# Hybrid block of delta-rule attention, feed-forward and selective scan: the places of all streams drawn anew

## The chip, the cores and the metric

The kernel runs on one core of a Trainium2 chip. The metric is the device time of one execution in microseconds. A core has a matrix engine (TensorE), VectorE, ScalarE and GpSimd for work on elements, and SyncE, which here starts the DMAs. In the profile they are PE (PEld for its weight loads), DVE, ACT, POOL and SP.

## What is computed

Four layers with residuals on x of 2 x 1024 x 256 in float32, each on a layer norm of x: a gated delta-rule attention with 16 heads, a feed-forward, a selective scan (state 16), and the same feed-forward again.

```python
# attention: per head q, k, v = silu(short_conv(x @ W)); q, k normalised
def step(S, inp):
    qt, kt, vt, gt, bt = inp
    S = S * gt[..., None]
    pred = jnp.einsum('bhk,bhkv->bhv', kt, S)
    delta = (vt - pred) * bt[..., None]
    S = S + kt[..., None] * delta[:, :, None, :]
    return (S, jnp.einsum('bhk,bhkv->bhv', qt, S))
...
x = x + attn_a(layernorm(x))            # 16 heads, 1024 steps
x = x + ffn(layernorm(x))               # silu(x Wg) * (x Wu), then Wd
x = x + attn_b(layernorm(x))            # h = dA * h + dt*u*B, y = sum(h * C)
x = x + ffn(layernorm(x))
```

## The kernel before

Time lies in two segments of 512 columns. The attention runs over 32 heads, g = 0 to 31 (16 heads of each segment). The work of a head is cut into thirteen streams: three convolutions (projection by TensorE L360, copies by ScalarE L931/932, three tap products by VectorE L670), `dots` (norms of q and k, L378, L682, L686, and `bs` in L692), `gating` (L395, L703, L986/988, L708, L992), `turn_v` (L406, L718), `products`, `inverse`, `turn_k` (L507/517, L812), `solved` (L532, L541), `out_gate` (L559), `state` (eight chunks, each L579/587 by TensorE, L842 by VectorE, L592 by TensorE, L847 by VectorE; L600 after four) and `output` (L863, L873, L617, L628, L885).

`products` works in five levels. At its start VectorE scales k by the gate (L732) and GpSimd scales q (L1165); GpSimd then makes `bm` (L1171) and `side` from `bs`. In each level TensorE multiplies (L425), then VectorE scales one half of `R` (L756, in the first level also `tot` in L747 and `kL` in L754) while GpSimd scales `kL` and the other half (L1187, L1190, L1192); VectorE cuts the result out of PSUM (L764, L766). `inverse` uses these in eight rounds of 32x32 products (L467, L487, L495) with ScalarE's copy (L1008) and VectorE's L788 and L798 between.

Each stream is a generator that yields between its steps, and it exists once for each engine with the same steps. `braid` runs the streams of an engine in the order of the places of their steps. The place of step k of a stream of head g is 100 (g + lag) + place, so 100 units are one head. Since every engine uses the same places, they set the order of the instructions in each engine's queue, and nothing else: what waits for what is in semaphores. A queue is in order, so an instruction that waits holds all that is behind it. TensorE takes its PSUM banks in turn from a ring of three, in the same order (`take`), and waits there until the bank's last reader is done.

In the last heads two feed-forward tiles (`EARLY_AT`, absolute places) are braided in. After a barrier of all engines (`all_over`) the tail begins: `tail_drive` braids four scans (100 units each, 64 items of a ScalarE exponential L1896, GpSimd's product L1987, VectorE's scan L1693 and product L1699, and TensorE's gathering L1512), four fronts that prepare them (`FRONT_FROM[u] + FRONT_AT`; L1614, L1621, L1629, L1639, L1664), and six feed-forward tiles (`FFN_FROM[w] + FFN_AT`; L1566, L1571, L1583, L1589).

```python
for stage, (lag, places) in zip(stages, PLACES):
    streams.append((stage(g), [100 * (g + lag) + at for at in places]))
...
streams.append((scan(u), [100 * (u + 1) + 100 * i / ITEMS for i in range(ITEMS)]))
streams.append((front(u), [FRONT_FROM[u] + at for at in FRONT_AT]))
```

## Time and profile before

| | us |
|---|---|
| median of 3 runs | 3098.76 (3098.74 to 3106.72) |
| the profiled execution | 3098.16 |
| its span, first to last instruction | 3096.4 |
| mean granted clock of TensorE | 0.934 of full |
| busy: PE, PEld | 2679.6 (87%), 1611.2 (52%) |
| busy: DVE, ACT, POOL | 2304.3 (74%), 1404.4 (45%), 1451.9 (47%) |

The profile gives each engine's busy time, and for the idle time in front of an instruction what ended it. "issue" there is time in which an engine waited for nothing that the profile shows. An engine's busy time counts an instruction from its start to its end, also the part in which it is held up by another engine.

### The profile page before, as it was taken

To read this page: it belongs to the slowest core of one execution; us is meant where nothing else is said; L and a number is where in the kernel's file an instruction comes from. 1 tells how busy PE (TensorE), PEld (TensorE's weight loads), DVE (VectorE), ACT (ScalarE), POOL (GpSimd) and SP (SyncE) were. 2 spreads that over 40 slices of the span, in tenths; PEclk is the share of its full clock that TensorE was granted. 3 is DMA by queue.
4 is the path that set the end of the run, shared out by engine and by line. 5 is a ranking of instruction groups with operands and counts; after the bars stand their busy time and mean duration, and the time that the engine had idled before them with its cause. 6 is when DMAs were issued, how large, how long until landed. Compare 5 with 4: busy or idle time off the path is not lost.

```text
span 3096.4 us, 119846 instructions
## 1 busy us (share of the span) xinstructions
PE 2679.6 (87%) x54704; PEld 1611.2 (52%) x54704; DVE 2304.3 (74%) x3249; ACT 1404.4 (45%) x2584; POOL 1451.9 (47%) x1245
## 2 busy tenths in 40 slices
PE   6788888988889888988988998888978889888889
PEld 3455556665666655666665666556433334333333
DVE  3677777877788877787877887775214999999992
ACT  3444444444454544454444544443326454635441
POOL 0534444444445444445444454443002887766760
PEclk8899989999899999999989999998989999989999
DMA  1000000000000000000000000001001332323330
GB/s 47 20 11 12 12 12 18 13 13 12 12 18 14 12 12 12 18 12 15 12 12 13 17 15 12 12 6 47 1 22 49 106 116 93 115 96 113 104 111 14
DMA packets 52137, 106.71 MB, mean 34 GB/s; under 512 B 7084, under 2 KB 11948, under 8 KB 51376
## 3 DMA queue, kind: packets, MB, share of 16 engines
q1 hardware_dynamic: 51632, 99.04, 9.9%
q8 instruction: 431, 7.06, 0.9%
q14 instruction: 74, 0.61, 0.1%
HBM read 96.65 MB, written 2.37 MB: 32 GB/s over the span
## 4 chain that ended last, share of the span: by engine, by line
PE 65%; DVE 16%; issue 11%; ACT 6%; DMA 0%; DVEq 0%; POOL 0%; SPq 0%; ACTq 0%; POOLq 0%
PE bank L360 10%; PE bank L467 9%; DVE hs L1693 5%; PE bank L628 4%; PE pair L592 3%; PE bank L425 3%; PE bank L395 3%; PE bank L1512 3%; DVE cv L670 3%; PE pair L579 3%; PE bank L1434 2%; PE bank L600 2%; PE bank L541 2%; PE bank L532 2%; PE pair L1434 1%
## 5 line engine op out<-in xcount | busy, mean ns | idle before, releaser
L670 DVE SCALAR_TENSOR_TENSOR cv<-raw,taps,cv 128x1024 f32<-128x1024 f32 x288 | 449.8, 1562 | 22.5 <-ACT cv L932 21.0
L1987 POOL TENSOR_TENSOR dBu<-dtu,Bn 128x512 f32<-128x512 f32 x256 | 377.8, 1480 | 62.8 <-DVE hs L1693 60.0
L360 PE MATMUL bank<-xn,W 128*128 128x512 f32 x768 | 401.1, 649 | 3.8 <-issue 3.8
L931 ACT ACTIVATE raw<-bank 128x512 f32<-128x512 f32 x192 | 114.8, 598 | 522.0 <-PE bank L360 522.0
L1190 POOL TENSOR_TENSOR kL<-kL,tot 128x512 f32<-128x512 f32 x128 | 188.5, 1473 | 345.6 <-PE bank L425 345.6
L1512 PE MATMUL bank<-hc,eye 128*128 128x512 f32 x512 | 271.2, 639 | 72.6 <-DVE hc L1699 72.0
L1896 ACT ACTIVATE bank<-dtv,m_A 128x512 f32<-128x512 f32 x256 | 173.7, 688 | 247.7 <-DVE hs L1693 243.0
L360 PEld LDWEIGHTS bank<-xn,W 128*128 128x128 f32 x768 | 144.3, 202 | 147.9 <-issue 123.6
L1512 PEld LDWEIGHTS bank<-hc,eye 128*128 128x128 f32 x512 | 93.1, 197 | 236.0 <-DVE hc L1699 158.8
L1192 POOL TENSOR_TENSOR R<-R,tot 128x512 f32<-128x512 f32 x128 | 212.5, 1661 | 0.0
L1699 DVE TENSOR_TENSOR hc<-hs,Cn 128x512 f32<-128x512 f32 x256 | 194.0, 758 | 8.8
L592 PE MATMUL pair<-vT,kT 64*128 64x128 f32 x1024 | 134.3, 341 | 43.2 <-DVE vT L842 43.2
L467 PE MATMUL bank<-XY,Z 32*32 32x32 f32 x8192 | 121.0, 206 | 57.0 <-issue 57.0
L847 DVE SCALAR_TENSOR_TENSOR Sx<-S,tot_chunk,pair 128x128 f32<-128x128 f32 x256 | 76.2, 339 | 124.9 <-PE pair L592 124.9
L1165 POOL TENSOR_TENSOR R<-qn,gate 128x1024 f32<-128x1024 f32 x32 | 77.5, 2421 | 194.3 <-ACT gate L992 194.3
L1693 DVE TENSOR_TENSOR_SCAN hs<-bank,carry,dBu 128x512 f32<-128x512 f32 x128 | 163.4, 1277 | 4.2 <-ACT bank L1896 3.3
L756 DVE TENSOR_TENSOR R<-R,tot 128x512 f32<-128x512 f32 x128 | 105.9, 827 | 78.9 <-PE bank L425 78.9
L425 PEld LDWEIGHTS bank<-R,kL 128*32 128x32 f32 x10240 | 118.3, 112 | 86.1 <-issue 78.5
L1693 DVE TENSOR_TENSOR_SCAN hs<-bank,dBu 128x512 f32<-128x512 f32 x128 | 155.7, 1216 | 8.8 <-ACT bank L1896 8.8
L425 PE MATMUL bank<-R,kL 128*32 128x64 f32 (+1 forms) x10240 | 139.9, 205 | 19.2 <-issue 8.8
L467 PE MATMUL bank<-Z,XY 32*32 32x32 f32 x8192 | 116.8, 203 | 43.7 <-issue 41.3
L592 PEld LDWEIGHTS pair<-vT,kT 64*128 64x128 f32 x1024 | 82.7, 198 | 130.5 <-DVE vT L842 63.5
(270 smaller groups left out, 6094.5 us busy)
## 6 DMA issues: line engine op xcount, KB each, us to landing
Bn<-ssm_rows SPq DMA_DIRECT2D x128, 256.0 KB, 3.5
Cn<-ssm_rows SPq DMA_DIRECT2D x128, 256.0 KB, 3.2
W<-in_head_w SPq DMA_DIRECT2D x32, 448.0 KB, 3.2
WO<-in_out_w SPq DMA_DIRECT2D x32, 192.0 KB, 2.3
xT<-in_xT SPq DMA_DIRECT2D x1, 2048.0 KB, 7.5
out_xT<-xT SPq DMA_DIRECT2D x4, 512.0 KB, 4.0
xn<-in_w_gate SPq DMA_DIRECT2D x1, 1024.0 KB, 5.7
xn<-in_w_up SPq DMA_DIRECT2D x1, 1024.0 KB, 8.5
```

The lines of the kernel that those rows point to most:

```text
L360: m = pe.matmul(psum[bank][:, :], w[:, (kind * KT + k) * P:(kind * KT + k + 1) * P], xn[:, k, b, cols], start=k == 0, stop=k == KT - 1)
L425: m = pe.matmul(o, block(kL[s], c, b, u), r)
L467: m = pe.matmul(psum[INV][quad(w), (at * NC + c) * SUBB:(at * NC + c + 1) * SUBB], lhsT[quad(w), c, :], rhs[quad(w), c, :])
L592: m = pe.matmul(psum[CHAIN[b]][:, P:2 * P], kT[s][rows_of(b), c, :], vT[g % 3][rows_of(b), c, :])
L670: dve.scalar_tensor_tensor(cv[m % 2][:, :, :], raw[m % 2][:, :, i:i + SEG], taps[:, h, KQV[n], i:i + 1], cv[m % 2][:, :, :], MUL, ADD).the ...
L1190: pool.tensor_tensor(Lv[:, :, 0, :], Lv[:, :, 0, :], spread(two[:, :, 1], 2, half), MUL).then_inc(up_l.sem)
L1192: pool.tensor_tensor(Rv[:, 1, :, 1, :], Rv[:, 1, :, 1, :], spread(two[:, :, 0], 2, half), MUL).then_inc(up_q.sem)
L1512: pe.matmul(psum[Y_BANKS[jj]][:, :], eye[:, :], hc[(u * ITEMS + i) % AHEAD][:, :], start=False, stop=n == NS - 1, skip_group_check=True).t ...
L1693: dve.tensor_tensor_scan(hs[at % NA][:, :], psum[A_BANKS[at % NA]][:, :], dBu[at % AHEAD][:, :], carry[:, b, i:i + 1] if seg else 0.0, MUL ...
L1699: dve.tensor_tensor(hc[at % AHEAD][:, :], hs[at % NA][:, :], Cn[at // DT2 % DEEP][:, :], MUL).then_inc(hc_set.sem)
L1896: act.activation(psum[A_BANKS[at % NA]][:, :], dtv[u % 2][:, j, :], ACT.Exp, scale=m_A[:, j, n:n + 1]).then_inc(dA_set.sem)
L1987: pool.tensor_tensor(dBu[at % AHEAD][:, :], dtu[s][:, j, :], Bn[at // DT2 % DEEP][:, :], MUL).then_inc(dBu_set.sem)
```

## The change

Only numbers change: the places of all thirteen attention streams, of the two early feed-forward tiles, and those of fronts and feed-forwards in the tail. The lags and the numbers of steps stay as they are. In `PLACES` the entries are, in order, the streams as listed above (convolutions of k, q, v; dots; gating; turn_v; products; inverse; turn_k; solved; out_gate; state; output). The change is described as places redrawn knowing that VectorE's two-operand SBUF products and GpSimd's instructions exclude each other.

```diff
@@
 PLACES = [
-    (0, [-1, 7.3, 19, 20.5, 26.9, 34.4]),
-    (0, [18.6, 27.2, 35.2, 42.1, 51.2, 58.1]),
-    (0, [40.1, 51.1, 52.9, 52.9, 59.8, 61.8]),
-    (0, [57.5, 62.1, 70.7, 83.3]),
-    (0, [66.3, 66.3, 70.5, 83.1, 83.8, 94.9]),
-    (0, [83, 89.7]),
-    (1, [1.4, 1.4, 2.9, 5.9, 12.5, 18.2, 28.2, 37.2, 41.7, 46.7, 57.2, 67.1, 73.2, 75.4, 78.4]),
-    (1, [13.2, 31.6, 33.3, 35.8, 39.7, 44.3, 47, 49.3, 49.4, 57.2, 59.8, 63.8, 67.2, 76.6, 76.6, 78.5, 81.5,
-         83.6, 83.9, 89.9, 94]),
-    (1, [78.5, 82.8, 83, 83]),
-    (1, [102.2, 102.5, 103.2]),
-    (2, [14.6, 16.3]),
-    (2, [10.5, 15.5, 16.4, 16.5, 20, 24.3, 29.2, 33.5, 35.6, 47.4, 51.7, 57.3, 59.8, 65.6, 69.9, 74, 78.4,
-         78.4]),
-    (2, [40.1, 40.1, 77.9, 79.2, 79.4, 82.3, 82.3, 89, 89.2, 93.2, 93.2, 98.2, 104]),
+    (0, [-8.5, 14.8, 26.1, 26.5, 30.8, 37.7]),
+    (0, [17.7, 29.9, 34.7, 36.4, 42.7, 42.9]),
+    (0, [40.6, 45.2, 57.6, 59.2, 64.4, 65.9]),
+    (0, [69.8, 71.7, 74.1, 101.1]),
+    (0, [54.3, 70.2, 79.9, 88.5, 90, 92.8]),
+    (0, [84.8, 87.3]),
+    (1, [-7.8, -5.8, 2.6, 13, 16.3, 17.1, 27, 30.8, 40.7, 43.6, 53.4, 55.2, 70.5, 73.6, 83.6]),
+    (1, [16.1, 20.3, 21.5, 30.7, 37, 42.2, 42.4, 48.8, 49.4, 56.4, 60.6, 60.6, 64.8, 71.2, 71.2, 74.3, 77.5,
+         78.6, 84.7, 89.9, 90.8]),
+    (1, [78.3, 80.4, 87.6, 91]),
+    (1, [94.4, 95.7, 100.8]),
+    (2, [11.5, 41.5]),
+    (2, [7.5, 14.1, 16.2, 17, 19.9, 26.2, 30.4, 35.9, 35.9, 47.9, 51.9, 53.6, 55.9, 57.6, 65, 71, 74.1, 75.2]),
+    (2, [31.2, 42.6, 76.4, 77.7, 81.8, 86.1, 87.8, 95.5, 96.3, 98.7, 106.3, 111.8, 119.6]),
 ]
@@
-FFN_AT = [-6.8, -5, -2.1, 1.9, 6.6, 8.8, 10.8, 17.9, 19.4, 22.5, 25.8, 39.4, 44.4, 48.1, 50.7, 53.6, 55.6, 59.8,
-          65.3, 69.1, 71.9, 75.5, 80.8, 84.2, 92.2, 99.6]
-FFN_FROM = [0, 0, 29.6, 149.1, 229.8, 347.3, 431.6, 515.9]
-FRONT_FROM = [-32.6, 87.5, 207.3, 307.1]
+FFN_AT = [-16.5, -9, -4.1, 11.5, 17.9, 21.5, 28, 28.3, 35.2, 36.9, 40.5, 47.4, 50.3, 51.9, 54.7, 55.2, 56.8, 58.5,
+          59.5, 61.4, 68, 72.6, 79.7, 91.4, 111.8, 220]
+FFN_FROM = [0, 0, 43.8, 141.1, 240, 340.5, 429.9, 519.6]
+FRONT_FROM = [-2, 102.3, 199.3, 299.2]
```

`FRONT_AT` (44 places, -11.4 to 89.8 before, -9.5 to 91.6 after) and `EARLY_AT` are replaced in the same way. In `EARLY_AT` tile 0 goes from 3306.3 to 3391.1 before, and from 3224.3 to 3447.1 after. Its sum, centring, squares and scaling stand at 3224.3 to 3260.2, its gate products at 3317.2 to 3337.4, its two down products at 3375.5 and 3382.5. Tile 1 goes from 3363.7 to 3475.4 before, and from 3355 to 3748.4 after; its eight gate products stand at 3392.4 to 3401.9 before, and from 3466.6 on after. The last step of the last head's output is at 3404 before and at 3419.6 after.

## Rows read from the trace of the kernel before

**Rows 1.** Windows of the stages: stretch, its length, each engine's busy time, clock, DMA.

```profile
62.00:2108.00 2046.00, 1798.82 (x51164) 1230.95 (x51162) 1592.93 (x2429) 961.61 (x1951) 936.57 (x793) 0.93 0.04 13
2108.00:2288.00 180.00, 159.88 (x1924) 90.03 (x1922) 64.77 (x122) 54.46 (x104) 26.34 (x21) 0.95 0.06 20
2288.00:2371.70 83.70, 56.52 (x104) 21.61 (x104) 21.63 (x29) 43.17 (x55) 8.39 (x11) 0.82 0.17 49
2371.70:2388.30 16.60, 15.45 (x32) 6.57 (x32) 6.28 (x7) 6.50 (x9) 8.14 (x6) 0.90 0.05 17
2388.30:3020.00 631.70, 539.15 (x1144) 212.68 (x1144) 587.15 (x631) 305.47 (x424) 471.63 (x404) 0.96 0.33 106
3020.00:3096.40 76.40, 69.84 (x162) 30.20 (x160) 14.56 (x21) 14.89 (x18) 0.00 (x0) 0.99 0.04 14
```

**Rows 2.** Waits of TensorE from 1000 to 2000 us: total, times, longest.

```profile
PE bank L467 <- issue: 38.8, 42, 1.8
PE pair L592 <- DVE vT L842: 21.9, 47, 1.3
PE bank L378 <- issue: 20.6, 15, 1.9
```

**Rows 3.** Timeline of TensorE: start, length, instructions, [idle before, releaser].

```profile
1019.49 0.45 PE L467 MATMUL bank<-XY,Z 32*32 32x32 f32 x30 [0.60 <-issue]
1019.87 1.98 PE L360 MATMUL bank<-xn,W 128*128 128x512 f32 x4
1021.78 0.76 PE L425 MATMUL bank<-R,kL 128*32 128x32 f32 x64
1022.47 0.44 PE L467 MATMUL bank<-XY,Bc 32*32 32x32 f32 x29
1023.26 0.50 PE L467 MATMUL bank<-XY,Bc 32*32 32x32 f32 x35 [0.34 <-issue]
...
1027.01 0.57 PE L467 MATMUL bank<-XY,Z 32*32 32x32 f32 x43 [1.81 <-issue]
...
1036.04 0.80 PE L592 MATMUL pair<-vT,kT 64*128 64x128 f32 x4 [1.32 <-DVE vT L842]
```

**Rows 4.** Windows before and behind the wait at 1036.04, columns as rows 1.

```profile
1027.00:1035.90 8.90, 6.37 (x315) 4.50 (x315) 7.54 (x8) 2.39 (x4) 4.47 (x4) 1.00 0.02 6
1036.00:1039.40 3.40, 3.36 (x140) 3.02 (x140) 3.02 (x6) 0.67 (x1) 0.00 (x0) 0.50 0.02 5
```

**Rows 5.** Groups by line and shape, VectorE: count, busy us, mean ns, idle before.

```profile
L670 DVE SCALAR_TENSOR_TENSOR cv<-raw,taps,cv 128x1024 f32<-128x1024 f32 x288 | 449.8, 1562 | 22.5 <-ACT cv L932 21.0
...
L747 DVE TENSOR_TENSOR tot<-gate 128x512 f32<-128x512 f32 x32 | 91.6, 2864 | 0.0
...
L732 DVE TENSOR_TENSOR R<-kL,gate 128x1024 f32<-128x1024 f32 x32 | 64.9, 2028 | 2.3 <-ACT gate L992 2.3
```

**Rows 6.** The instructions of L670: fastest, median and slowest, in ns.

```profile
L670 DVE SCALAR_TENSOR_TENSOR cv<-raw,taps,cv x288: 1269/1283/2194, 59.0 to 2084.5; 128x1024 f32<-128x1024 f32 x144
```

**Rows 7.** Timeline of GpSimd and VectorE around the `bm` product of one head.

```profile
1058.03 3.77 POOL L1171 TENSOR_TENSOR bm<-masks,bs 128x1536 f32<-128x1536 f32 x1
...
1059.42 2.92 DVE L747 TENSOR_TENSOR tot<-gate 128x512 f32<-128x512 f32 x1
1062.27 0.70 DVE L754 TENSOR_TENSOR kL<-kL,gate 128x512 f32<-128x512 f32 x1
```

**Rows 8.** Group by line and shape, TensorE's output product.

```profile
L628 PE MATMUL bank<-WT,WO 128*128 128x512 f32 x256 | 128.2, 623 | 0.0
```

**Rows 9.** Timeline of VectorE and ScalarE ahead of the first scan.

```profile
2363.71 1.23 DVE L1664 TENSOR_TENSOR dtv<-dtv,cen 128x1024 f32<-128x1024 f32 x1 [5.12 <-ACT cen L1882]
...
2385.73 2.69 DVE L1629 SCALAR_TENSOR_TENSOR un<-cen,m_norm,m_rstd 128x512 f32<-128x512 f32 x2
2388.35 1.21 DVE L1693 TENSOR_TENSOR_SCAN hs<-bank,dBu 128x512 f32<-128x512 f32 x1
...
2370.36 1.28 ACT L1763 ACT_TABLE_LOAD   x1
```

More of the change, by code:

```diff
@@ L54 @@
 ]
 FRONT_STEPS, FFN_STEPS = 44, 26
-FRONT_AT = [-11.4, -9.5, -6.6, -6.6, -0.4, 0.5, 6.8, 6.8, 7.5, 12.4, 14.9, 17.5, 17.9, 17.9, 18.3, 18.3, 19.4, 19.9,
-            20.6, 20.6, 21.9, 44.6, 44.6, 44.6, 44.6, 45.9, 51, 57.3, 59.6, 63.6, 64.6, 66.2, 67.9, 74.8, 75.2,
-            76.7, 77.5, 77.7, 80.6, 81.2, 85.9, 85.9, 86.4, 89.8]
-FFN_AT = [-6.8, -5, -2.1, 1.9, 6.6, 8.8, 10.8, 17.9, 19.4, 22.5, 25.8, 39.4, 44.4, 48.1, 50.7, 53.6, 55.6, 59.8,
-          65.3, 69.1, 71.9, 75.5, 80.8, 84.2, 92.2, 99.6]
@@ L61 @@
-FFN_FROM = [0, 0, 29.6, 149.1, 229.8, 347.3, 431.6, 515.9]
-FRONT_FROM = [-32.6, 87.5, 207.3, 307.1]
+FRONT_AT = [-9.5, -4, -1.2, 1.7, 4, 6.1, 8.8, 10.7, 14.4, 14.7, 15.8, 17.8, 17.8, 18.2, 18.3, 18.3, 18.3, 18.3,
+            18.5, 18.5, 18.8, 18.8, 18.8, 18.8, 18.8, 19.3, 19.9, 19.9, 26.9, 28.9, 40.3, 48.3, 52.1, 55.4, 59.2,
+            59.2, 59.2, 65.7, 67.9, 74.4, 75, 88, 90.5, 91.6]
+FFN_AT = [-16.5, -9, -4.1, 11.5, 17.9, 21.5, 28, 28.3, 35.2, 36.9, 40.5, 47.4, 50.3, 51.9, 54.7, 55.2, 56.8, 58.5,
+          59.5, 61.4, 68, 72.6, 79.7, 91.4, 111.8, 220]
```

8 rows, old and new, of the table EARLY_AT are left out of this document.

## Prediction

> **What bounds the kernel now.** I read the stages first. Thirty-two heads take most of the span, then come a drain, a short stretch up to the first selective scan, four scans, and an end [rows 1]. From 62 to 2108 us TensorE is busy 1798.8 of 2046 us (88%) and VectorE 1592.9 (78%): the matmul queue sets the pace, the other engines matter only where it waits for them. From 2388.3 to 3020 the order is reversed: VectorE is busy 587.2 of 631.7 us (93%).
>
> Second, the waits of TensorE from 1000 to 2000 us, some fifteen heads (L378, one of its gaps in each head, counts 15) [rows 2]. The two rows that name no other engine (short matmuls of L467 and L378) come to 59.4 us, 4.0 us a head; the wait for VectorE's `vT` before L592 is 21.9 us, 1.5 a head. In all TensorE idles (2046 - 1798.8)/31.4 = 7.9 us a head from 62 to 2108 us [rows 1], so some 2.4 us are left for every other wait.
>
> Third, the timeline of TensorE in one head [rows 3]. The gaps without a releaser start at 1019.49, 1023.26 and 1027.01, 3.77 and 3.75 us apart. Between the first two lie 30+4+64+29 = 127 matmuls, each with one weight load, so about 256 instructions. The queue cannot take them faster than 256 in some 3.76 us: a run of 32-column matmuls, 64 of which need 0.69 us (from 1021.78 to 1022.47), outruns it. The wait of 1.32 us for `vT` follows in the same head, and right behind it the granted clock is 0.50 for 3.4 us where it was 1.00 before, the lower of its two levels (1.2 and 2.4 GHz) [rows 4]. So a bunched idle costs more than its own length: a 3.4 us stretch at half clock does the work of 1.7 us.
>
> Fourth, what VectorE and GpSimd cost each other. L670 takes 1.56 us on the mean [rows 5], 1.28 as the median and up to 2.19 [rows 6]: 288 x 0.28 = 80 us over the run. L747 takes 2.86 us [rows 5]. In one head it starts at 1059.42 and ends only 0.54 us after GpSimd's `bm` product (1058.03 to 1061.80) has; the same shape behind it, L754, takes 0.70 [rows 7]. L732 takes 2.03 [rows 5]. All that is VectorE's time, in a stretch where VectorE has 22% to spare.
>
> **The change.** No instruction is added or removed; only places move, so every term below is a wait. I sorted the steps of each engine by their places, modulo one head, before and after.
>
> *VectorE and GpSimd within a head.* After the level products (L756 with GpSimd's L1190, L1192) the new order puts VectorE's work on PSUM (L842, L847, L764/766, L885) where a two-operand SBUF product (L670, L788) stood. That takes part of the 80 us away from L670. What counts is TensorE's 1.5 us a head before L592 [rows 2], most of it the wait at 1036.04 [rows 3]. I take half of it, -0.7 us a head; one bound is that all of it and 1 us of the other waits go (-2.5), the other is the loss of the next paragraph.
>
> *The step that sets `bs` (L692)* moves from 83.3 to 101.1, behind L732, L737 and the first L885. GpSimd has L1171 (`bm`) at 94.2 and waits there for `bs`; behind it in its queue stand `side`, the first L1192 and the next head's halo copies, and the second L425 product waits for L1192. L747 then goes ahead of `bm` and loses its stall (about 2.86 - 0.70 = 2.2 us), but L754 meets `bm` in flight, up to 3.77 us [rows 7]. TensorE's cover until it needs VectorE (L592 of chunk 0) is two L628 products of two matmuls, 4 x 0.623 = 2.5 us [rows 8], an out-gate product and L579. So 0 to 1.3 us a head; I take 0, since the two L628 do not count the other two, and TensorE still has L541 and L425 in front of L754.
>
> *TensorE's order.* Short matmuls (L425, L434, L455, L467, L378, L487, L495) are 1376 a head in both. Before, 672 lie between the second v projection and the next head's first; now 800. The longest stretch between two projections, up to the second L600, now holds 736 short ones and 68 others, 804 in all, 1608 instructions, 6.3 blocks of 256: at 3.76 us each 23.6 us, less one block's head start 19.8. Its own work is 804 x 6.37/315 = 16.3 us by the busy time of a like mix [rows 4], and some 15 if the short ones run at the 0.69 us for 64 of rows 3. That is 3.5 to 4.9 us of gaps; the other half of the head (576 short ones between four projections) then has next to none, where before the gaps of rows 3 stood. Against 4.0 now that is -0.5 to +0.9; I take the middle, +0.2. Sum for a head: -0.7 + 0 + 0.2 = -0.5, times 31 = **-15 us**; bounds -2.5-0.5 and +1.3+0.9 a head, -93 to +68.
>
> The Trainium skill (Runtime: NRT & Kernel Launch, Instruction fetch mechanics) says that instructions stream in blocks of 256 and that crossing a block is mostly hidden. The spacing of rows 3 agrees with the size of the block; that it is hidden does not hold here, by 4.0 us a head. By the page the term of TensorE's order would be nothing and the sum -0.7 a head, -22 us.
>
> *The other queues.* ScalarE's exp/ln of the gate go from 83.1 to 88.5 and the last exp from 94.9 to 92.8, the second tanh from 16.3 to 41.5; the ring of three banks is handed on in the new order. ScalarE is busy 47% of this stage [rows 1]; I cost these at nothing. If a bank comes late, a projection waits: inside the bounds above.
>
> *The drain (2108 to 2288 us, TensorE idle 20 us [rows 1]).* Feed-forward tile 0 starts at 3224 instead of 3306, so its norm chain hides. Tile 1's eight gate products go from 3392 to 3402 to behind the last head's output (3466 on): 16 matmuls of about 0.6 us, 10 us, no longer fill that head's norm, but tile 0's down products now do. I take **-4 us**, bounds -12 and +10.
>
> *From the barrier to the scans.* Before, ten steps of front(1) stood ahead of scan(0): VectorE's L1629 at 2385.73, then the first scan at 2388.35, although `dt` was ready at 2363.71 + 1.2 and ScalarE was through with silu and its table at 2371.6 [rows 9]. FRONT_FROM[1] goes from 87.5 to 102.3, so two steps stand ahead, and of tile 2 sixteen steps instead of twenty. The scan can start at about 2371.7, 16.6 us earlier. VectorE did 6.3 us of work in those 16.6 [rows 1], which moves into a stage that VectorE bounds: **-10 us**. Bounds: 0 and -16 for this, and +-10 for how the 44.5 us that VectorE idles in the scans [rows 1] change; front(1) now ends at 193.9, six units ahead of scan(1), where it had 23. The moved output stores sit later in SyncE's queue, where nothing waits for them; the order of the last 76 us is the same.
>
> Sum: 3098.16 (the profiled execution, 1.8 us above its span of 3096.4, and 0.6 below the median of 3098.76) - 15 - 4 - 10 = **3069**.
>
> **Rivals.** (A) *Only the tail moves.* TensorE's queue sets the head whatever VectorE does; VectorE's 22% of slack swallows its stalls. For it: the 59.4 us against 21.9 in rows 2. The heads stay, the drain too: 3098 - 10 = 3088, from 3075 to 3100.
>
> (B) *The stalls reach TensorE and its clock.* With the 1.3 us waits gone (1.5 us a head), the half-clock stretch of rows 4 goes too (1.7 us): 3.2 x 31 = 99, with drain and tail 113: 2985. Against it: the gaps of 1.8 and 1.3 us without a releaser stay, in a longer run.
>
> (C) *`bm` behind `bs`, in the bunched run: slower.* L754 held for the whole of `bm` and TensorE reaching L592 first: 1.3 us a head, from the point where `bm` starts after L747 and outlasts TensorE's 2.5 us; plus half of the 0.9 us of the longer run of short matmuls: 1.7 x 31 = 53 - 14 = +39: 3137, and 3124 with the first alone. For it: every cover in that place is TensorE's alone, and 736 short matmuls in one stretch.
>
> (D) *The change does not do what it says:* VectorE meets GpSimd as often as before, only elsewhere (L754 for L747). Then the time is as (A), and it counts there; the busy time of VectorE tells them apart.
>
> The Trainium skill (SBUF — State Buffer, the engine and AXI sides) has the shared port pair as an exclusive lock, held for the full instruction, which the one that starts first gets. L747, which ends 0.54 us after `bm`, agrees; by that, L754 would wait for nearly the whole of `bm`, which is (C).
>
> **How the numbers follow.** The forecast 0.40, (A) with (D) 0.22, (B) 0.13, (C) 0.25. Some 0.3%, 9 us, is what a measurement here can tell from no change: faster means under 3089.5. The forecast gives 0.37 faster and 0.03 same; (A) half and half; (B) faster; (C) 0.03 same and 0.22 slower. Together faster 0.61, same 0.17, slower 0.22. For 8 in 10 I leave out the far half of (B) and the far end of (C): 2992 to 3132.
>
> **What would show it.** L747 near 0.7 us and L754 above 1.2: the `bs` step as described. L670's mean under 1.45: the port relief is real. TensorE's wait before L592 under 1 us a head: the gain term. The gaps without a releaser 3.5 to 4.9 us a head and bunched between the v projections and L507: the block reading; fewer, and it was wrong. The first L1693 some 16 us nearer to the barrier: the tail term. I would be wrong most simply if a head's mean length changed by over 1.5 us either way.

## Result: 2976.6 us, 4% faster, below the forecast range

| | before | after |
|---|---|---|
| median, us | 3098.75 (3095.6 to 3106.72, 4 runs) | 2976.56 (2969.01 to 2989.22, 4 runs) |
| ratio | | 0.9606, 95% interval 0.9568 to 0.9644 |
| profiled execution, its span | 3098.16, 3096.4 | 2969.01, 2967.2 |
| TensorE's mean granted clock | 0.934 | 0.956 |

The forecast was 3069, with a range from 2992: the sign was right, the gain is four times the 29 us of the sum. The profiled execution of the changed kernel is the fastest of its four, at the highest clock (the median of the four is 0.9535). Lines of the changed kernel are one lower than before's (L669 is L670 of before).

The stages of the changed kernel, columns as rows 1: the heads, the drain, from the drain to the first scan, the scans, the end.

```profile
62.00:2012.00 1950.00, 1745.45 (x51056) 1185.92 (x51054) 1442.77 (x2417) 944.67 (x1929) 880.72 (x791) 0.96 0.05 14
2019.80:2201.70 181.90, 163.04 (x1937) 89.07 (x1936) 64.63 (x127) 58.94 (x111) 26.33 (x21) 0.97 0.06 20
2201.70:2281.00 79.30, 56.64 (x111) 22.35 (x112) 21.11 (x29) 45.38 (x57) 13.08 (x15) 0.85 0.19 55
2281.00:2887.30 606.30, 537.52 (x1174) 216.46 (x1173) 587.81 (x637) 313.23 (x433) 476.99 (x406) 0.98 0.34 111
2887.30:2967.20 79.90, 70.31 (x157) 29.64 (x156) 15.69 (x22) 14.89 (x18) 0.00 (x0) 0.98 0.04 13
```

Of the 129.2 us between the two spans the heads (first L434 of head 0 to first L434 of head 31, 2027.7 and 1943.3 us) carry 84, the stretch from the drain to the first scan 20 (100.5 and 80.1), the scans 23 (629.1 and 606.2) and the fill 4; drain and end are 2 and 1 us longer. In the scans, fourth line against the fifth of [rows 1], VectorE is busy 587.8 us as before, but its idle time falls from 44.5 to 18.5 us. The drain ends, and the stretch to the first scan begins, with the start of the last residual sum ahead of the tail (L1589 of before, at 2287.85 and 2201.02 us).

The waits of TensorE from 1000 to 2000 us in the changed kernel, the four longest and one more (before: [rows 2]):

```profile
PE bank L377 <- issue: 24.1, 15, 1.9
PE bank L424 <- issue: 22.8, 15, 1.9
PE bank L466 <- issue: 17.7, 19, 1.8
PE pair L591 <- DVE vT L841: 6.0, 15, 0.4
...
PE bank L466 <- DVE XY L797: 4.0, 16, 0.3
```

The wait for `vT` falls from 21.9 to 6.0 us, 0.4 us a head. The idle time that names no other engine does not fall: these three rows are 64.6 us, where the two of [rows 2] were 59.4. It moves. (Where `issue` is named, the gap had no releaser.) In the timeline of TensorE its gaps now stand in one stretch of the head, behind the second v projection:

```profile
1047.84 0.35 PE L466 MATMUL bank<-Z,XY 32*32 32x32 f32 x19 [0.43 <-issue]
...
1051.15 0.41 PE L377 MATMUL bank<-kL 128*32 128x32 f32 x26 [1.49 <-issue]
...
1055.00 0.44 PE L586 MATMUL bank<-Sx,R 128*64 128x128 f32 x4 [0.44 <-issue]
...
1058.84 0.27 PE L466 MATMUL bank<-Z,XY 32*32 32x32 f32 x9 [1.57 <-issue]
```

Windows of one head show both halves, in the changed kernel first the stretch with the short matmuls, then the one with the projections:

```profile
1035.00:1066.00 31.00, 25.76 (x898) 17.95 (x896) 17.83 (x36) 11.91 (x29) 7.07 (x8) 0.94 0.06 19
1066.60:1099.00 32.40, 31.71 (x725) 20.19 (x727) 26.75 (x42) 17.37 (x34) 19.37 (x15) 1.00 0.03 9
```

and in the kernel before:

```profile
1027.50:1056.30 28.80, 25.24 (x783) 18.30 (x776) 24.35 (x39) 15.54 (x33) 11.00 (x11) 0.94 0.06 20
1056.30:1090.60 34.30, 30.41 (x880) 20.78 (x878) 27.57 (x40) 15.17 (x30) 20.74 (x16) 1.00 0.03 9
```

The half with the projections is now busy 98% (31.71 of 32.4 us), where it idled 3.9 us. Counted over 15 heads, 83 of the 84 us of gaps without a releaser lie in one stretch of some 900 matmuls; before they were 33 us in two stretches of some 270 matmuls between projections and 31 us in the longest.

VectorE's products by line and shape (before: [rows 5], and for L754 [rows 7]), then the fastest, median and slowest L669 (before: [rows 6]), and GpSimd's `bm`:

```profile
L669 DVE SCALAR_TENSOR_TENSOR cv<-raw,taps,cv 128x1024 f32<-128x1024 f32 x288 | 398.6, 1393 | 20.5 <-ACT cv L931 17.9
...
L753 DVE TENSOR_TENSOR kL<-kL,gate 128x512 f32<-128x512 f32 x32 | 65.0, 2030 | 37.0 <-PE bank L424 37.0
L731 DVE TENSOR_TENSOR R<-kL,gate 128x1024 f32<-128x1024 f32 x32 | 39.2, 1225 | 40.7 <-ACT gate L991 40.7
...
L746 DVE TENSOR_TENSOR tot<-gate 128x512 f32<-128x512 f32 x32 | 21.7, 679 | 0.0
```

```profile
L669 DVE SCALAR_TENSOR_TENSOR cv<-raw,taps,cv x288: 1268/1279/2371, 58.7 to 1999.8; 128x1024 f32<-128x1024 f32 x144
```

```profile
L1170 POOL TENSOR_TENSOR bm<-masks,bs 128x1536 f32<-128x1536 f32 x32 | 101.0, 3156 | 3.5
```

L746 loses its stall (2.86 to 0.68 us) and L753 gets one (0.77 to 2.03 on the mean). VectorE's busy time falls from 51.5 to 46.6 us a head. So the change does on VectorE what it says, though single L669 are still held (the slowest took 2371 ns).

**Two terms make a head.** For the 26 heads from the fifth on I added up, from the instructions and from the clock records, TensorE's idle time and the time at the lower of its two clock levels (0.50 of full in [rows 4]). "Rest" is the length less the idle time less half of the low-clock time: what the work would take at full clock, if a microsecond at half clock cost half a microsecond.

| us per head | length | idle | of it no releaser / VectorE | at low clock | rest |
|---|---|---|---|---|---|
| before | 65.24 | 7.17 | 4.74 / 2.10 | 8.27 | 53.9 |
| after | 62.89 | 6.14 | 5.23 / 0.61 | 4.73 | 54.4 |

Of the 2.35 us that a head loses, 1.03 are idle time and 1.32 busy time at a better clock. That split is of one pair of executions, and it varies. The same heads also ran in kernels that changed nothing in them (told of below), and each series of runs had a chip of its own:

| us per head | length | idle | no releaser / VectorE | at low clock | low stretches in 26 heads |
|---|---|---|---|---|---|
| old heads: before | 65.24 | 7.17 | 4.7 / 2.1 | 8.27 | 41 |
| tail alone (chip A) | 65.69 | 7.82 | 5.6 / 1.8 | 7.88 | 36 |
| front 1 alone (chip B) | 65.98 | 7.90 | 5.8 / 1.7 | 8.27 | 40 |
| front 1 and tile 2 (chip C) | 65.94 | 7.79 | 5.6 / 1.8 | 8.53 | 41 |
| new heads: after | 62.89 | 6.14 | 5.2 / 0.6 | 4.73 | 27 |
| heads alone (chip A) | 63.43 | 6.53 | 5.6 / 0.6 | 4.99 | 31 |
| after, again (chip B) | 63.94 | 6.31 | 5.4 / 0.6 | 6.96 | 35 |

A head gains 2.35, 2.26 (chip A) and 2.04 us (chip B). Of this, idle time is 1.03, 1.29 and 1.59, and busy time at a better clock 1.32, 0.97 and 0.45. So both terms are real, and which is the larger is not settled. The idle time without a releaser changes by +0.5, 0 and -0.4; the waits for VectorE fall in all three, by 1.2 to 1.5.

Eighteen of the traced executions, all but the two with more short matmuls (below), have the same matmuls in their heads. Over them TensorE's busy time a head is 55.2 us plus 0.35 us for every microsecond at low clock, to within 0.15 us. The price of low clock is thus nearer to a third of it than to half; the "rest" (53.7 to 54.7 us) drifts for that reason.

### The profile page after: what moved, and what is told of

Read it like the earlier page. It is cut to its first block, busy times and chain, and to the rows that moved or that the text cites. A ratio compares the mean times of both kernels' runs of the same rounds, so it can differ in the third digit from the quotient of the medians.

```text
span 2967.2 us, 119848 instructions
## 1 busy us (share of the span) xinstructions
PE 2619.1 (88%) x54704; PEld 1568.7 (53%) x54704; DVE 2153.5 (73%) x3249; ACT 1400.7 (47%) x2586; POOL 1399.0 (47%) x1245
## 4 chain that ended last, share of the span: by engine, by line
PE 62%; DVE 20%; issue 12%; ACT 4%; POOL 1%; DMA 0%; DVEq 0%; SPq 0%; ACTq 0%; POOLq 0%
PE bank L359 9%; PE bank L466 7%; DVE hs L1692 7%; DVE cv L669 6%; PE bank L627 4%; PE bank L394 3%; PE bank L1511 3%; PE bank L424 3%; PE pair L578 3%; PE pair L591 2%; PE bank L531 2%; PE bank L540 2%; PE bank L1433 2%; PE bank L377 2%; PE bank L599 2%
## 5 line engine op out<-in xcount | busy, mean ns | idle before, releaser
L669 DVE SCALAR_TENSOR_TENSOR cv<-raw,taps,cv 128x1024 f32<-128x1024 f32 x288 | 398.6, 1393 | 20.5 <-ACT cv L931 17.9
L1986 POOL TENSOR_TENSOR dBu<-dtu,Bn 128x512 f32<-128x512 f32 x256 | 379.0, 1484 | 53.9 <-DVE hs L1692 53.3
L359 PE MATMUL bank<-xn,W 128*128 128x512 f32 x768 | 381.8, 621 | 0.0
L1189 POOL TENSOR_TENSOR kL<-kL,tot 128x512 f32<-128x512 f32 x128 | 179.1, 1399 | 242.7 <-PE bank L424 242.7
L1164 POOL TENSOR_TENSOR R<-qn,gate 128x1024 f32<-128x1024 f32 x32 | 108.6, 3392 | 284.6 <-ACT gate L991 284.6
L1191 POOL TENSOR_TENSOR R<-R,tot 128x512 f32<-128x512 f32 x128 | 192.3, 1502 | 0.0
L359 PEld LDWEIGHTS bank<-xn,W 128*128 128x128 f32 x768 | 132.4, 192 | 111.8 <-issue 101.9
L1207 POOL TENSOR_TENSOR kL<-kL,tot 128x512 f32<-128x512 f32 x32 | 33.8, 1055 | 292.5 <-PE bank L454 292.5
L424 PE MATMUL bank<-R,kL 128*32 128x64 f32 (+1 forms) x10240 | 137.9, 204 | 35.8 <-issue 27.5
L755 DVE TENSOR_TENSOR R<-R,tot 128x512 f32<-128x512 f32 x128 | 126.5, 988 | 48.3 <-PE bank L424 48.0
L841 DVE TENSOR_TENSOR vT<-vT,pair 128x128 f32<-128x128 f32 x256 | 72.1, 282 | 118.3 <-PE pair L578 115.0
L424 PEld LDWEIGHTS bank<-R,kL 128*32 128x32 f32 x10240 | 116.4, 111 | 76.3 <-issue 65.1
L884 DVE TENSOR_TENSOR xT<-xT,bank 128x512 f32<-128x512 f32 x128 | 87.7, 685 | 80.2 <-PE bank L627 78.4
L1086 ACT ACTIVATE cen<-bank 128x128 f32<-128x128 f32 x256 | 67.4, 278 | 164.4 <-PE bank L599 164.4
```

The source lines that it names most:

```text
L359: m = pe.matmul(psum[bank][:, :], w[:, (kind * KT + k) * P:(kind * KT + k + 1) * P], xn[:, k, b, cols], start=k == 0, stop=k == KT - 1)
L424: m = pe.matmul(o, block(kL[s], c, b, u), r)
L669: dve.scalar_tensor_tensor(cv[m % 2][:, :, :], raw[m % 2][:, :, i:i + SEG], taps[:, h, KQV[n], i:i + 1], cv[m % 2][:, :, :], MUL, ADD).the ...
L1189: pool.tensor_tensor(Lv[:, :, 0, :], Lv[:, :, 0, :], spread(two[:, :, 1], 2, half), MUL).then_inc(up_l.sem)
L1191: pool.tensor_tensor(Rv[:, 1, :, 1, :], Rv[:, 1, :, 1, :], spread(two[:, :, 0], 2, half), MUL).then_inc(up_q.sem)
L1986: pool.tensor_tensor(dBu[at % AHEAD][:, :], dtu[s][:, j, :], Bn[at // DT2 % DEEP][:, :], MUL).then_inc(dBu_set.sem)
```

## Experiments

Each ratio is against the kernel before on the same chip, with its 95% interval; "clock" is the median, over the runs, of the mean granted clock, with that of before in the same series. The changed kernel in its own first series has 0.9535 (before's profiled run 0.934).

**The two halves of the change.** Heads alone (`PLACES` of after in the kernel before; its lines are one lower too) and tail alone (`FRONT_AT`, `FRONT_FROM`, `FFN_AT`, `FFN_FROM` of after in the kernel before); `EARLY_AT` stays old in both.

> The kernel before with the new PLACES alone. From the two traces 84 of the 129 us lie in the thirty-one heads, 44 in the tail. If the two parts are independent: about 3099 - 84 = 3015, the end of the attention as before. If part of what the heads gained came from the early feed-forward's new places: above 3025.

> The kernel before with the new FRONT_AT, FFN_AT, FFN_FROM and FRONT_FROM alone. If the tail is independent of the heads: 3099 - 44 = 3055 (20 us from the barrier to the first scan, 23 in the scans). My prediction had 10 in all: 3089.

Measured: heads alone 0.9819 (0.9796 to 0.9843), 56 us; tail alone 0.9861 (0.9825 to 0.9898), 43 us. Together that is 0.968; the missing 0.8%, 24 us, is mostly the drain: with the new heads and the old `EARLY_AT` it takes 200.2 us, with the new one 181.2, 19 us less. In the tail alone the first scan comes 18 us nearer and the scans last 606.2 us, as in the changed kernel. The heads themselves (first L434 to first L434) take 2044.2 us in the tail alone and 1959.4 in the heads alone, on one chip: 85 us, as in the first pair. VectorE's idle time in the scans goes with the tail's places only: 18.5 us in the tail alone, 44.5 in the heads alone.

**The v taps.** In the kernel before, four places of the v convolution moved behind the last level's L756, where the new order has them; in the changed kernel, the first two tap products back in front of it.

```diff
-    (0, [40.1, 51.1, 52.9, 52.9, 59.8, 61.8]),
+    (0, [40.1, 51.1, 57.4, 59.9, 63, 65]),
```

```diff
-    (0, [40.6, 45.2, 57.6, 59.2, 64.4, 65.9]),
+    (0, [40.6, 45.2, 52, 52.1, 64.4, 65.9]),
```

> The kernel before with one stream changed, on VectorE and ScalarE's silu only: the three tap products of v (L670) go from 52.9, 52.9, 59.8 to 57.4, 59.9, 63, behind the last level's L756. TensorE's order is untouched. Theory 1 (VectorE held at the port makes TensorE wait for vT at L592, and that wait drags the clock): the 1.3 us wait goes, and with it a half-clock stretch in many heads; 1.3 to 3 us a head, 3000 to 3060. Theory 2 (TensorE's own order made the gain): within 10 us of 3099.

> The kernel after with the first two tap products of v brought back in front of the last level's L756 (57.6, 59.2 to 52, 52.1), as they stood before. Theory 1: they meet GpSimd's fourth level, L756 and the vT products are late, and TensorE waits again: 1 to 3 us a head, 3005 to 3070. Theory 2: within 10 us of 2977.

Measured: late in the old order 1.0014 (0.9993 to 1.0036), clock 0.9345 against 0.934. Early in the new order 0.9843 (0.9817 to 0.9868) where the changed kernel has 0.9606: 74 us lost, clock 0.9335. (The 74 us are the difference of the two ratios, 0.0237 of 3099.) TensorE's waits from 1000 to 2000 us in the first kernel, two of its rows:

```profile
PE bank L467 <- issue: 65.9, 50, 2.2
...
PE pair L592 <- DVE vT L842: 6.5, 30, 0.3
```

The wait for `vT` is gone as far as in the changed kernel (21.9 to 6.5), and nothing is won: L467 waits 65.9 us without a releaser where it waited 38.8 [rows 2], and 50.0 in the tail alone on this kernel's chip. The reading is that in the old order the wait for VectorE lay inside a run of short matmuls that was held anyway. In the new order the same collision costs: against the heads alone, on one chip, idle time goes from 6.53 to 7.53 us a head and low clock from 5.0 to 9.3 us. The row of the second kernel is

```profile
PE pair L591 <- DVE vT L841: 14.6, 21, 3.5
```

**Port contention taken away.** GpSimd's two level products only write; the values of the level products are left out.

```diff
-                        pool.tensor_tensor(Lv[:, :, 0, :], Lv[:, :, 0, :], spread(two[:, :, 1], 2, half),
-                                           MUL).then_inc(up_l.sem)
-                    pool.tensor_tensor(Rv[:, 1, :, 1, :], Rv[:, 1, :, 1, :], spread(two[:, :, 0], 2, half),
-                                       MUL).then_inc(up_q.sem)
+                        pool.memset(Lv[:, :, 0, :], 0.01).then_inc(up_l.sem)
+                    pool.memset(Rv[:, 1, :, 1, :], 0.01).then_inc(up_q.sem)
```

> The kernel before, in which GpSimd fills its level tiles (L1190, L1192) with a constant instead of multiplying them: it writes the same tiles at the same places and reads nothing, so the attention's values are not the reference's. Theory 1 (what holds L670, L756, L788 up is GpSimd's reading of SBUF): L670's mean falls from 1.56 to about 1.3 us, L756 and L788 to their fastest. If the whole wait for VectorE (2.1 us a head) were of that, it would go; but v_late showed that the waits without a releaser take such a gain back: 0 to 2 us a head, 3050 to 3113 on this chip, where before is 3113.

> The kernel after, in which GpSimd fills its level tiles with a constant instead of multiplying them (the attention's values are not the reference's). In the kernel before this took 5.0 us of VectorE's busy time a head and 1.3 us of TensorE's waits for it, and the time stayed: its waits for instructions rose by 1.5. Theory (TensorE is held by its instruction blocks in both, the port costs nothing where it is hidden there): within 10 us of after again. Rival (in the new order TensorE is free of the blocks and the port is the bound): 1 us a head or more, 30 us under after again.

Measured: 0.9979 (0.9959 to 0.9998) in the kernel before, and 0.9584 (0.9549 to 0.9619) in the changed one, whose own ratio in that series is 0.9631 (`after_again`, below). Three rows of the kernel before so edited, L670's spread and two waits of TensorE from 1000 to 2000 us:

```profile
L670 DVE SCALAR_TENSOR_TENSOR cv<-raw,taps,cv x288: 1264/1279/1423, 59.1 to 2081.6; 128x1024 f32<-128x1024 f32 x144
```

```profile
PE bank L467 <- issue: 63.0, 49, 2.2
...
PE pair L592 <- DVE vT L842: 7.0, 32, 0.3
```

The slowest L670 falls from 2194 to 1423 ns [rows 6], the slowest L756 from 2007 to 700, and VectorE works 5 us less a head, so the level products were what held it. (The constant also takes GpSimd only 0.52 us where the product took some 1.5, so it is beside VectorE for less time; that no L756 of 160 was held speaks against this as the whole reason.) TensorE turns the relief into gaps without a releaser (6.21 us a head, where the old heads have 4.7 to 5.8). The contention of the level products is worth 0.2% in the old order and some 0.5% in the new (medians 2985.8 and 3001.6 us in one series, whose ranges do not meet).

The Trainium skill (SBUF — State Buffer, SBUF: two separate sides) says that the shared pair of ports goes for a whole instruction to the one that starts first. L753 agrees. In one head of the changed kernel it comes while `bm` runs and ends 0.55 us after it, as L747 did in [rows 7] (0.54):

```profile
1074.72 3.16 POOL L1170 TENSOR_TENSOR bm<-masks,bs 128x1536 f32<-128x1536 f32 x1
...
1076.35 2.08 DVE L753 TENSOR_TENSOR kL<-kL,gate 128x512 f32<-128x512 f32 x1 [1.10 <-PE bank L424]
```

L753 loses only 1.3 us on the mean, and not nearly all of `bm` as (C) had it: it first waits for TensorE's L424 while `bm` is running.

**The step that sets `bs`.**

```diff
-    (0, [69.8, 71.7, 74.1, 101.1]),
+    (0, [69.8, 71.7, 74.1, 87]),
```

> The kernel after with the step that sets bs (L692) at 87 instead of 101.1. In the trace of after VectorE's L754 takes 2.03 us on the mean (0.77 before) and L692 0.71 (0.16 before), L747 is free. Theory: with bs early, GpSimd's bm goes first, L747 is held for 2 us again and L754 is free, a change of place with the same sum; TensorE has cover in both: within 10 us of after (2990 on this chip). If the bs step was what freed TensorE, 1 us a head or more comes back: over 3020.

Measured: 0.963 (0.9594 to 0.9666), clock 0.952; the changed kernel has 0.9606 and 0.9631 in its two series. The step is worth nothing that can be told. Two groups of this kernel:

```profile
L753 DVE TENSOR_TENSOR kL<-kL,gate 128x512 f32<-128x512 f32 x32 | 61.8, 1933 | 40.1 <-PE bank L424 40.1
...
L746 DVE TENSOR_TENSOR tot<-gate 128x512 f32<-128x512 f32 x32 | 38.9, 1216 | 0.0
```

L746 and L753 cost 3.15 us together with the early place and 2.71 with the late one, on an engine with slack. (The place tried is 87, not the 83.3 of before; L746 is held there for about 0.5 us and not for 2.)

**Are the gaps tied to 256 instructions?** A count of matmuls put once ahead of the heads, 64 more in the records (128 with their weight loads) for `range(32)`, 32 for `range(16)`:

```diff
+            pe.wait_ge(eye_loaded.sem, 16)
+            for _ in range(32):
+                m = pe.matmul(psum[1][0:SUBB, 0:SUBB], eye[0:SUBB, 0:SUBB], eye[0:SUBB, 0:SUBB])
             m.then_inc(logits_full.sem)
```

> The same 128 instructions ahead of the heads of the kernel before. Block theory: the gaps inside L467 and L378 move by 64 matmuls; walking both orders in blocks gave 7.4 us a head for before where it stands, and 8.8 on the mean over all positions, so this is more likely to cost than to gain: 0 to 45 us more than before. Rival: gaps and time stay.

> The kernel after with 32 small matmuls more (64 matmuls and 64 weight loads, 128 instructions) before the first head. Block theory: every gap without a releaser sits where a block of 256 instructions begins, so it moves by 64 matmuls in the program, from inside L377 and L424 to other groups; the sum a head changes by up to 1 us either way, the total by up to 40 us. Rival (these gaps are waits of certain instructions that the profile doesn't name): they stay at the same instructions of a head, and the time within 5 us of after.

> The kernel after with 64 instructions more ahead of the heads. A walk through its order in blocks of 256 instructions, each at least 3.75 us, gives 6.8 us a head of gaps here, 7.1 for after and 7.7 with 128 instructions more (which cost 0.46 us a head in the trace). So 0.2 to 0.3 us a head less than after: 5 to 10 us faster, if the blocks set it; no difference if not.

Measured: 1.0079 (1.0048 to 1.0109), 0.9642 (0.9612 to 0.9672) and 0.9669 (0.9631 to 0.9706). The padding takes under a microsecond of its own, yet the kernel before gets 24 us slower. In the trace its heads last 66.78 us, with 7.91 us idle and 10.37 us at low clock, the highest low-clock time of all kernels with these matmuls. TensorE's timeline in the padded kernel before (L470 and L428 are L467 and L425), the head of rows 3:

```profile
1012.26 0.50 PE L470 MATMUL bank<-Z,XY 32*32 32x32 f32 x34
1013.13 0.42 PE L470 MATMUL bank<-Z,XY 32*32 32x32 f32 x28 [0.38 <-issue]
...
1015.97 0.45 PE L428 MATMUL bank<-R,kL 128*32 128x32 f32 x29
1017.10 0.51 PE L428 MATMUL bank<-R,kL 128*32 128x32 f32 x35 [0.68 <-issue]
...
1018.81 0.38 PE L470 MATMUL bank<-Z,XY 32*32 32x32 f32 x21
1021.29 0.66 PE L470 MATMUL bank<-Z,XY 32*32 32x32 f32 x42 [2.10 <-issue]
```

In [rows 3] a gap stood after 29 of the 64 matmuls of L467 that follow 64 of L425. Here it stands after 29 of those 64 of L425: 64 matmuls earlier in the code, which is the padding. The gap goes with the count of instructions, not with any matmul. The distances say the same: over some three heads of the kernel before and of the changed one, the gaps stand 127 or 128, 254 or 255, 382 or 383, 509 and 758 matmuls apart, close to one, two, three, four and six times 127, each matmul with its weight load.

A calculation of mine walks the written order in blocks of 256 instructions and lets each last at least 3.75 us. It gives for the kernel before 7.35 us of gaps a head at its own starting point and 9.5 to 10 with the padding (8.8 on the mean of all starting points); for the changed kernel 7.10, 7.7 and, with the small padding, 6.8 (mean 7.2). These are not measurements, and they lie above the 4.7 to 5.8 us in the traces. The large sign came true: before is slower with the padding. For the changed kernel the large padding shows nothing clear of the difference between two series (0.9642 against 0.9606 and 0.9631). The small one was to win 0.2 to 0.3 us a head and lost: 3013.0 us (from 3004.5) against 3001.6 (up to 3003.1) for the changed kernel in the same series.

**The changed kernel again**, in another series, as the measure for its variants:

> The kernel after, unchanged, beside the others of this set: 0.961 of before.

Measured: 0.9631 (0.9595 to 0.9667), clock 0.9475 against 0.933. Two series of one kernel differ by 0.25%, with the clock on the same side.

**More short matmuls**, inside the long run (the products of L378 twice) and outside it (L434 three times):

> The kernel before with its dots products (L378, 128 short matmuls) made twice, into the same place: 128 matmuls and 128 loads more a head, one block of 256 instructions, inside the run in which the gaps without a releaser stand. If TensorE's own work were the price: 128 x 0.011 = 1.4 us a head, 45 us. If the run is bound by the blocks: one block more, 3.75 us a head, 120 us.

> The kernel before with its first product of a head (L434, 64 short matmuls) made three times: the same 128 matmuls and loads more a head, between a projection and L532, where no gap without a releaser stands. Blocks: it takes its own work, 1.4 us a head, 45 us, or a little more where a new gap opens. If instructions cost the same everywhere, it is as the run before it.

Measured: 1.0375 (1.0337 to 1.0413) and 1.031 (1.0261 to 1.036). By the medians, against the kernel before in the same series, that is 117 and 99 us, 3.8 and 3.2 us a head. The forecast that outside the run they would cost 1.4 us failed. But this does not tell inside from outside: three times L434 are 192 matmuls in a row, a run of its own, in which L434 waits 24.9 us without a releaser. What it shows is the price. 128 more short matmuls have about 1.4 us of work and cost more than twice that: 256 more instructions are one block of 3.75 us.

**The short run spread.** The direct test, in the kernel before: four places, the same work.

```diff
-    (0, [66.3, 66.3, 70.5, 83.1, 83.8, 94.9]),
+    (0, [60, 66.3, 70.5, 83.1, 83.8, 94.9]),
@@
-    (1, [13.2, 31.6, 33.3, 35.8, 39.7, 44.3,
+    (1, [13.2, 21.6, 23, 25, 39.7, 44.3,
```

> The kernel before with four places of an attention head moved: three steps of the inverse from 31.6, 33.3, 35.8 to 21.6, 23, 25, and the first gating step from 66.3 to 60. The same work. It breaks up the run of short TensorE instructions between the projection of v and the decay's line. Theory (the gaps without a releaser come one to every 256 TensorE instructions, and cost time only where 256 instructions last less than 3.75 us of TensorE's work): walking the written order in blocks of 256 at each of the starting points gives a mean of 7.2 us of such gaps a head for this order against 8.8 for the kernel before, so 1 to 1.6 us a head less, 30 to 50 us on 31 heads, of which waits for VectorE may take back a half: 3050 to 3090 us, ratio 0.984 to 0.997. Rival (the positions of short instructions don't matter; the gain of the changed kernel is its waits for VectorE alone): within 0.3% of the kernel before.

> The kernel before with both the four places of spread and the late v taps of v_late (57.4, 59.9, 63, 65 in place of 52.9, 52.9, 59.8, 61.8), which were worth nothing by themselves (1.0014). Theory (the waits for VectorE lay inside the run that was bound by the blocks of instructions, so taking them away can only pay once that run is spread): 0.5 to 1.5% below spread alone, the wait for vT under 0.8 us a head and the idle time without releaser lower than v_late's 6.5 us. Rival (the two don't act on each other): the same as spread, within 0.3%.

Measured: 0.9858 (0.9817 to 0.9898), and with the late v taps 0.9797 (0.976 to 0.9834); medians 3077.7 and 3058.7, with no run of one inside the range of the other. Four places give a third of the whole gain, and the v taps, worth nothing alone, give 19 us on top. The theory had named the idle time, 1 to 1.6 us a head less. The traces show the gain elsewhere for the most part:

| us per head | length | idle | no releaser / VectorE | at low clock | low stretches in 26 heads | clock, before's |
|---|---|---|---|---|---|---|
| before | 65.24 | 7.17 | 4.74 / 2.10 | 8.27 | 41 | |
| v late | 65.68 | 7.94 | 6.50 / 1.13 | 7.61 | 40 | 0.9345, 0.934 |
| spread | 64.43 | 7.29 | 4.97 / 1.96 | 5.25 | 33 | 0.9475, 0.932 |
| spread, v late | 64.04 | 7.28 | 5.78 / 1.15 | 4.20 | 26 | 0.955, 0.932 |
| after | 62.89 | 6.14 | 5.23 / 0.61 | 4.73 | 27 | 0.9535, 0.934 (one run) |
| after, v early | 65.93 | 7.53 | 4.94 / 2.29 | 9.32 | 41 | 0.9335, 0.934 |

These rows are from several chips, and no trace of the old heads is from spread's. The idle time of spread, 7.29 us, lies inside the 7.17 to 7.90 of the four executions of the old heads, so a fall of up to 0.6 us is possible and none is shown. The low-clock time, 5.25 us, lies far outside their 7.88 to 8.53. The clock of the windows from 1000 to 2000 us, before and then spread, is 0.94 and 0.97.

```profile
1000.00:2000.00 1000.00, 892.65 (x25090) 612.91 (x25088) 787.66 (x1210) 470.72 (x961) 465.53 (x371) 0.94 0.05 13
```

```profile
1000.00:2000.00 1000.00, 887.59 (x25889) 605.88 (x25890) 810.79 (x1233) 479.82 (x980) 478.06 (x377) 0.97 0.05 14
```

What differs for certain is where the gaps lie. Of the 41 low-clock stretches of the kernel before, 18 begin in L467 and 20 in L592: at the gaps of the first half of the head, and at the place where a gap in front of L378 and the wait for `vT` follow each other:

```profile
1098.70 0.75 PE L378 MATMUL bank<-qn 128*32 128x32 f32 x63 [1.37 <-issue]
...
1100.48 0.49 PE L592 MATMUL pair<-vT,kT 64*128 64x128 f32 x4 [1.02 <-DVE vT L842]
```

In spread 7 and 10 are left at these lines, and in the changed kernel 13 of 27 begin in one place, L377. The old heads, with two groups of idle time, have 36 to 41 low-clock stretches in 26 heads; the new ones, with one, have 27 to 35, and spread with late v taps has 26. That the stretches are fewer with the new grouping is measured; that the grouping is the cause is my reading, and which part of it the clock answers to was not tried.

**A further gain by the walk?** In the changed kernel one step of the inverse moved:

```diff
-    ... 60.6, 60.6, 64.8, 71.2, 71.2, 74.3, 77.5,
+    ... 60.6, 60.6, 64.8, 71.2, 71.2, 76.3, 77.5,
```

> The changed kernel with one step of the inverse moved from 74.3 to 76.3, behind the second part of the q gating. The same work. Theory (blocks of 256): the walk gives 6.7 us a head for the mean of all starting points against 7.2 for the changed kernel, so 0.2 to 0.5 us a head less, 6 to 15 us: 2961 to 2971 us where the changed kernel takes 2976.6, a ratio of 0.956 to 0.959. Rival (the place doesn't matter): the same as the changed kernel within the 0.4% by which its two series of runs differ (0.9606 and 0.9631).

Measured: 0.9608 (0.9561 to 0.9654), clock 0.945: the same as the changed kernel. The changed kernel did not run in this series. With the small padding, which went the other way, this is the second fine forecast of the walk that was not borne out. It is of no use for parts of a microsecond a head.

**The tail.** `FRONT_FROM[1]` alone from 87.5 to 102.3, then with `FFN_FROM[2]` from 29.6 to 43.8:

> The kernel before with FRONT_FROM[1] alone at 102.3 instead of 87.5. My forecast's mechanism (ten steps of front 1 stand ahead of the first scan): the first scan starts 15 to 17 us sooner after the attention's end, the scans take some 6 us more, together -10: 3088 where before is 3098. The whole new tail brought 20 and 23. If the 23 of the scans come of the same move, the scans get shorter here too: below 3080.

> The kernel before with FRONT_FROM[1] at 102.3 and FFN_FROM[2] at 43.8. Front 1 alone moved the first scan only 9 us nearer and made the scans 20 us longer. If feed-forward tile 2 (twenty of its steps ahead of the scan, now sixteen) held the other part of the start: the first scan 15 to 20 us nearer. If the longer scans came of front 1 meeting that tile, they are back at 629 or less; if front 1 ending nearer to scan 1 costs by itself, they stay at about 649.

Measured: 1.0039 (1.0017 to 1.0061) and 1.0031 (1.001 to 1.0052). The first alone brings the scan 9 us nearer (100.5 to 91.5 us) and makes the scans 20 us longer (629.1 to 648.8); the second 1 us farther and 9 us longer. VectorE's waits in the scans, three rows of the kernel before (2388.3 to 3020 us):

```profile
DVE hs L1693 <- ACT bank L1896: 12.1, 9, 3.3
DVE xT L1679 <- PE pair L1519: 7.9, 4, 3.6
DVE sq L1571 <- ACT f_rstd L1743: 4.2, 4, 1.9
```

and of the changed kernel (2281 to 2887.3 us):

```profile
DVE xT L1678 <- PE pair L1518: 2.5, 2, 1.7
DVE hs L1692 <- ACT bank L1895: 2.4, 3, 1.3
DVE sq L1570 <- ACT f_rstd L1742: 1.6, 2, 0.8
```

The same waits, at a fifth to two fifths of their size: together 24.2 and 6.5 us, so two thirds of the 26 us of idle time that went. The two starts do not explain it, since they made the scans longer. Which of the other new places does it, of fronts or of feed-forwards, was not tried, so the cause of this part stays open.

## Why the prediction missed the size

**What bounds the kernel: right.** TensorE's queue sets the heads, and its gaps come with 256 instructions: the padding moved them by just the matmuls that it added.

**Port relief: right on VectorE, too small by half on TensorE.** L670's mean went to 1.39 us (said: under 1.45), and the wait before L592 to 0.4 us a head (said: under 1). The term was half of 1.5 us, 0.7; all the waits for VectorE fell by 1.2 to 1.5 (2.10 to 0.61 in the first pair). The reason behind it was incomplete: v late, and the kernel with a writing GpSimd, take the same wait away in the old order for next to nothing. (A) was right for the old order, with its argument that the queue takes back what VectorE gives.

**The `bs` step: right.** L746 at 0.68 and L753 at 2.03 us are as described (about 0.7, and above 1.2), and undoing it changes nothing that can be told. So (C) failed at its condition: L753 is held for 1.3 us on the mean, and TensorE's L592 does not wait for it (0.4 us at the longest, from 1000 to 2000 us).

**TensorE's order: right in kind.** The gaps stand bunched between the v projections and L507, 5.2 to 5.6 us a head, just above the 3.5 to 4.9 foretold. The 4.0 from which the forecast started were two rows of waits only; all gaps of this kind in that trace are 4.7. Against the old heads they change by -0.4 to +0.5, where the sum had +0.2.

**The step that failed is the sum of a head, -0.5 us, in two of its terms.** Measured were -2.0 to -2.35. First, the idle time: -1.0 to -1.6 us, since the waits for VectorE were mis-sized. Second, the clock: the sum priced every term as idle time and so put it at nothing. The prediction had said that "a bunched idle costs more than its own length" and had a row for it [rows 4], but put it into rival (B) alone, as something that goes with the wait for `vT`. It does not go with that wait alone: in spread the low-clock time is 3.0 us a head less while the wait is still there (1.96 of 2.10), and in v late the wait is gone and the low-clock time hardly less (7.61 against 7.88 on one chip). In the changed kernel the low-clock time falls by 1.3 to 3.5 us and the busy time by 0.45 to 1.32 us a head. In the first pair that is 31 x 1.3 = 41 us for the clock and 31 x 0.53 = 16 us for the idle time. Of the 84 us less the 15 foretold that leaves 12, which lie in the first heads and the last. That half clock costs half was wrong too: over eighteen executions it costs 0.35, and why it is not more stays open.

**(B)** was the nearest in total, 2985 us, and it alone had the clock in it. That it comes within 9 us is luck. It had 3.2 us a head, measured are 2.0 to 2.35; and it had drain and tail as in the forecast (14 us), measured are 41. Its condition was not enough either: in the old order the wait went and nothing was won (1.0014). It got 0.13, since I held against it that the gaps without a releaser stay. They stay, but no longer in both halves of the head. **(D)** is refuted by VectorE's busy time, 51.5 to 46.6 us a head.

**The drain:** +2 us instead of -4, inside the bounds. The new `EARLY_AT` saves 19 us against the old one under the new heads, but what it saves is a loss that these heads bring.

**The tail:** the first scan is 20.4 us nearer (said: 16.6), right. The 6.3 us of moved work did not lengthen the scans: VectorE is busy 587.8 us there against 587.2. And its idle time, set at +-10 us, fell by 26. So the tail is mis-sized as well, 43 us instead of 10, by its term for VectorE's idle time. The edits on which the term rested are, `FRONT_FROM[1]` alone and with `FFN_FROM[2]`, slower than before; what it needs is among the other places of the tail, and which of them stays open.

## To carry to other kernels

A queue that is held by its own instruction supply can hide a wait that falls into the held run. Here spreading the short instructions first and then removing the wait paid, while the removal by itself measured as nothing (1.0014 alone, 19 us behind the spread). Count the time at low clock beside the idle time, and price an order by both; here a microsecond at low clock cost 0.35 us. Take the two traces that you compare from one chip, or several of each: the same heads had 7.2 to 7.9 us of idle time, a difference as large as some effects read here. Before a small re-ordering is believed, shift the same code by some dozens of instructions: 128 moved a kernel by 0.8%, and 64 the changed one by 0.4%.

## What the runs showed of the hardware

TensorE's supply: the gaps without a releaser stand 256 instructions of the queue apart, or a multiple of that, matmuls and weight loads together, with gap ends 3.31, 3.85 and 3.84 us apart in the changed kernel's stretch shown above (3.77 and 3.75 in [rows 3]). 128 instructions added once, ahead of 32 heads, cost 24 us in one order and nothing that can be told in the other; 64 cost 11 us there.

The clock: the changed kernel has 0.9535 at 2976.6 us in one series and 0.9475 at 3001.6 us in another, and within the first its executions go from 2969.0 us at 0.956 to 2989.2 us at 0.945. The order goes with as much: on one chip 0.932 for the kernel before and 0.955 for spread with late v taps.

A microsecond at half clock cost TensorE 0.35 us of busy time, over eighteen executions with the same matmuls in a head.

GpSimd's filling with a constant did not hold up VectorE's two-operand products: the slowest L670 took 1423 ns beside it, and 2194 beside products that read; the slowest L756 0.70 us and 2.01.
